# Side work on VectorE moved from in front of the row minimum to behind it, with one kind of task left in place

## The reference

```python
# 1. token encoder: embedding, e2h, six gated convolutions of width 3, h2e
for i in range(6):
    a, g = split(conv1d_same(x, conv_w[i], conv_b[i]))
    x = (a * sigmoid(g) + x) * 0.7071
h = x.T @ W_h2e + b_h2e
# 2. two attentions of 8 heads (16 wide), mixed by a gate
xn = layernorm(h)
attn1 = softmax(q1 @ k1.T / 4);  attn2 = softmax(q2 @ k2.T / 4)
stats = mean, std, max and min over windows of 4 rows of attn1 and attn2
alpha = sigmoid(mlp(stats))
h = h + (alpha * attn1 + (1 - alpha) * attn2) @ v @ Wo
# 3. normed mixture-of-experts style feed-forward
x = layernorm(layernorm(h)) * ln_g + ln_b ...;  h = h + gelu(fc2(gelu(fc1(x))) @ next_w)
```

## Time and profile before

| | |
|---|---|
| median of 3 runs | 5952.06 us (5943.18 to 5953.85) |
| the profiled execution: its own time | 5952.66 us |
| its span, first to last instruction | 5950.7 us |
| mean granted TensorE clock | 0.947 |
| TensorE matmul busy | 5237.1 us, 88% |
| VectorE busy | 5105.1 us, 86% |
| ScalarE busy | 5201.0 us, 87% |
| GpSimd busy | 2445.9 us, 41% |

### The profile page before, as it was taken

The page is one execution under the profiler, slowest core; times in us unless marked ns, Lnnn a source line. Parts: engine busy times, 40 slices in busy tenths (PEclk is TensorE's granted clock), DMA queues, the critical chain, the costliest instruction groups (busy, mean ns, idle before and its releaser), DMA issues.

```text
span 5950.7 us, 121038 instructions
## 1 busy us (share of the span) xinstructions
PE 5237.1 (88%) x34070; PEld 2513.5 (42%) x34070; DVE 5105.1 (86%) x7715; ACT 5201.0 (87%) x7937; POOL 2445.9 (41%) x4439
## 2 busy tenths in 40 slices
PE   6988989899898988989889898988989899898985
PEld 4443434444343443434344343443435344343443
DVE  2989899898998989899888988989899898989982
ACT  2998989889898999989889898998989889898893
POOL 6525344252433525344352434425353352534422
PEclk8999999999999999999999999999999999999996
DMA  1011010011101001010010101001010110101010
GB/s 38 19 23 27 18 31 20 21 27 24 27 20 29 20 21 27 20 31 19 22 28 22 27 20 28 20 23 27 22 27 20 24 24 21 27 20 30 18 23 10
DMA packets 164934, 140.87 MB, mean 24 GB/s; under 512 B 89197, under 2 KB 108269, under 8 KB 164141
## 3 DMA queue, kind: packets, MB, share of 16 engines
q1 hardware_dynamic: 159100, 124.09, 9.1%
q0 software_dynamic: 4352, 8.92, 0.7%
q10 hardware_dynamic: 816, 0.02, 0.0%
HBM read 21.26 MB, written 8.91 MB: 5 GB/s over the span
## 4 chain that ended last, share of the span: by engine, by line
PE 43%; ACT 24%; issue 15%; DVE 8%; POOL 6%; SPq 1%; ACTq 1%; DMA 1%; POOLq 0%; DVEq 0%
PE ps_w L389 19%; PE ps_t L389 10%; ACT junk L579 10%; ACT exps L586 8%; PE ps_o L389 8%; PE ps_s L389 6%; DVE neg_s L715 4%; DVE rowmin L723 2%; ACT hpre L590 2%; SPq L330 1%; DVE bn L735 1%; POOL part L866 1%; POOL ctmp L998 1%; POOL part L1000 1%; ACT L579 1%
## 5 line engine op out<-in xcount | busy, mean ns | idle before, releaser
L715 DVE TENSOR_SCALAR_CACHE_REDUCE neg_s<-ps_s 128x1024 f32<-128x1024 f32 x2048 | 2492.3, 1217 | 464.2 <-PE ps_s L389 399.0
L579 ACT ACTIVATE junk<-neg_s,negmax 128x1024 bf16<-128x1024 f32 x2048 | 2358.8, 1152 | 227.6 <-DVE neg_s L715 222.6
L723 DVE TENSOR_REDUCE rowmin<-neg_s 128x1 f32<-128x1024 f32 x2049 | 2467.3, 1204 | 0.0
L586 ACT ACTIVATE exps<-ps_t 128x1024 f32<-128x1024 f32 x2060 | 2112.6, 1026 | 171.2 <-PE ps_t L389 166.5
L389 PE MATMUL ps_t<-qst,kst 99*128 99x512 bf16 x4120 | 1300.6, 399 | 441.3 <-ACT exps L586 436.9
L389 PE MATMUL ps_o<-exps,v_cur 128*32 128x256 f32 x16512 | 1365.3, 404 | 133.2 <-DVE o_raw L731 112.2
L389 PE MATMUL ps_s<-kst,qst 96*128 96x512 bf16 x4096 | 1272.0, 392 | 65.3 <-DMA kst<-part 49.2
L389 PE MATMUL ps_w<-xc,cw 128*128 128x256 f32 x4704 | 1199.3, 392 | 1.0
L389 PEld LDWEIGHTS ps_w<-xc,cw 128*128 128x128 f32 x4704 | 922.4, 197 | 229.8 <-ACT chan L590 8.9
L866 POOL TENSOR_SCALAR ctmp<-ug 128x256 f32<-128x256 f32 x408 | 164.7, 404 | 1593.3 <-ACT ug L655 1577.9
L389 PEld LDWEIGHTS ps_t<-qst,kst 99*128 99x128 bf16 x4120 | 237.3, 98 | 1369.3 <-ACT exps L586 771.3
(11 more groups left out here) (181 smaller groups left out, 4031.4 us busy)
## 6 DMA issues: line engine op xcount, KB each, us to landing
qst<-part SPq DMA_DIRECT2D x1542, 32.0 KB, 2.0
kst<-part SPq DMA_DIRECT2D x1542, 32.0 KB, 2.0
qst<-mrow SPq DMA_DIRECT2D x1028, 1.5 KB
out_dram<-z SPq DMA_DIRECT2D x17, 512.0 KB, 3.2
fc1s<-in_fc_w SPq DMA_DIRECT2D x17, 256.0 KB
fc2s<-in_fc_w SPq DMA_DIRECT2D x17, 256.0 KB
cw<-in_conv_w SPq DMA_DIRECT2D x1, 2304.0 KB
odif<-in_table,idx POOLq DMA_INDIRECT x136
```

What stands on the lines that cost most here:

```text
L579: nc.scalar.activation(junk[:, n % 2, :], neg_s[:, n % SLOTS_S, :], ACT.Exp, scale=-1.0, bias=negmax[:, r, t:t + 1], accum_out=sumsq[:, r, ...
L586: nc.scalar.activation(exps[:, n % RING, :], ps_t[:, :, :].rearrange("p c q -> p (c q)"), ACT.Exp, scale=0.5).then_inc(s_exp, 1)
L715: nc.vector.tensor_scalar(neg_s[:, n % SLOTS_S, :], ps_s[:, n % 2, :], -1.0, None, ALU.mult, ALU.min, accum_out=negmax[:, r, t:t + 1]).the ...
L723: nc.vector.tensor_reduce(rowmin[:, r, t:t + 1], neg_s[:, m % SLOTS_S, :], axis=AX, op=ALU.max, negate=True).then_inc(s_min, 1)
```

## The change

In VectorE's loop the tasks of kind `unit` stay between `row_max` and `row_min`; all others of the step now come behind `row_min`. `plan` sorts the tasks of each step so that a `unit` stands first.

```diff
@@ plan
     for j in range(1, U + 1):
         at[j * T - 2].append(("msplit", j))
+    for n in range(STEPS):
+        at[n].sort(key=lambda task: task[0] != "unit")
     return at
@@ VectorE's loop
                     for n in range(STEPS):
                         row_max(i, n)
                         for tk in STEP[n]:
-                            task("body", i, tk)
+                            if tk[0] == "unit":
+                                task("body", i, tk)
                         row_min(i, n)
+                        for tk in STEP[n]:
+                            if tk[0] != "unit":
+                                task("body", i, tk)
```

## The result

The changed kernel takes 5885.93 us (median of 4 runs, 5878.64 to 5888.73), the kernel before on the same chip 5949.48 us (4 runs, 5943.18 to 5953.85). The ratio is 0.9892, with a 95% interval of 0.9875 to 0.9909: 1.1% faster, 63.6 us by the medians. The forecast was 5900 us, a gain of 52.3. One of nine runs of the kernel before, beside experiments 5 to 8, took 7499.44 us at a mean granted clock of 0.737 (the others 0.947 to 0.951); it is left out everywhere.

What follows compares the result with a forecast made beforehand. No engine bounds the whole, so waits were judged step by step: gains of 12.3, 13.7, 17.0, 6, 3 and 3.3 less a loss of 3 make 52.3 us, from 5952.7 to 5900 us; 8-in-10 range 5872 to 5936.

Steps and rivals of the forecast that it cites:

- Step 39, `wo`: VectorE's `wo` waits 0.77 us for TensorE; the minimum fills it all and the gain is kept: 12.3 us.
- Step 103, `h2e`: VectorE's 0.86 us wait at `h2e` goes entirely, VectorE being the pace until step 110: 13.7 us gained.
- Step 120: `mrow` waits for GpSimd near the batch's end; GpSimd's chain comes 1.06 us sooner a batch: 17.0 us gained.
- Step 8: `mrow` behind the gathering; ScalarE is the later engine in most batches: 6 us gained, bounds 0 and 16.
- Steps 16, 48, 96: `mrow`'s remaining 4 us of waits; ScalarE waits for VectorE behind 16 and 48, not 96: 3 us gained.
- `v`: Steps 123 and 124: bank freed about 1.1 us later, TensorE stands, ScalarE's spare time in step 125 covers it: 0.
- `snap` and the gate: Step 16's late reciprocal is covered by 2.0 us of slack; in steps 23 to 27 VectorE isn't the pace: 0 each.
- `next`: Step 89: 3.3 us in 16 VectorE waits, all before ScalarE's second GELU, are gained.
- the clock comes back too: Rival: TensorE's idle time before step 0 shrinks, steps 0 and 1 run at upper clock: 5883 us, chance 0.14.
- The end of the batch swallows: Rival: VectorE doesn't move the load of unit 0, so steps 103 and 120 gain nothing: 5931 us, chance 0.13.
- VectorE is covered: Rival: TensorE is the bound where VectorE idles, so only `next` and small `mrow` steps gain: 5949 us, chance 0.09.
- The bank: Rival: moved tasks free `ps_w` later and TensorE stands at `v`, `alpha` and `next`: slower, 5980 us, chance 0.07.

Runs made afterwards that it cites:

- experiment 5: The kernel before, with only `wo`, `h2e` and what stands in their steps moved behind the minimum: 5914.89 us against 5947.75, ratio 0.9948.
- experiment 6: The kernel before, with `mrow` moved behind the minimum in steps without another task, plus step 48 with `ln3`: 5924.84 us against 5947.75, ratio 0.9961.
- experiment 7: The changed kernel with both halves of `next` (steps 89 and 90) in their old place: 5866.65 us against 5947.75 before, ratio 0.9858.
- experiment 8: The changed kernel with `next` (steps 89, 90) and `v` (steps 123, 124) in their old place: 5869.24 us, ratio 0.9867 to the kernel before.
- experiment 3: The kernel before, with only the gate's `win`, `hid1` and `hid2` moved behind the minimum: 5946.66 us against 5945.66, ratio 1.0001.
- experiment 11: The kernel of experiment 7 with the norm `ln1` moved from step 108 to 109, behind that step's collection: 5871.34 us, ratio 0.9868 to the kernel before.
- experiment 9: The changed kernel with only the first half of `next` (step 89) in its old place: 5867.15 us against 5945.23 before, ratio 0.9869.

## Why the prediction was right, and where it was not

The total came out right with two terms wrong in opposite directions; that they nearly cancel is luck.

- *Step 39, `wo`* (12.3): 0.84 us a batch, 13 us. *Step 103, `h2e`* (13.7): 0.92 a batch, of which 0.23 is given back at step 112, 11 us. Together 24, and 32.9 us alone in experiment 5. Right, for the reason given: the squares behind the norms still wait 2.39 us for VectorE.
- *Step 120* (17.0): 1.10 us a batch, 17.6 us. The limit by GpSimd was the right one: `part` went from 1.30 to 0.24, the 1.06 of the forecast. `mrow` keeps 1.28 us there, some 20 in 16 batches, as forecast (19). *Step 8* (6): 0.41 a batch, 6.6 us. *Steps 16, 48, 96* (3): step 48 brings 0.29 a batch, 4.6 us, and the size is luck. Of the 4 us of waits that the forecast put here, 3.2 lie at step 96, where by its own words ScalarE doesn't wait, 0.8 at step 48 (two batches) and none at step 16. Step 48 gets shorter in every batch, from 4.93 to 4.67 us between row maxima, which the list of waits doesn't show. `mrow` alone, without step 16: 22.9 us against the forecast's 25.
- *`alpha`* (a loss of 3): nothing is lost; the shift doesn't move behind step 32. *`v`* (0): right, experiment 8.
- *`snap` and the gate* (0 and 0): here a step failed. I followed the late `snap` to ScalarE's `std` and found 2.0 us of slack, and I wrote down that the collection of step 21 would wait 1.2 us for GpSimd (it waits 1.3), but called that harmless and did not follow it to TensorE's `weighted` of step 22 and its clock. It gives 16 to 17 us. The sentence that the batches repeat each other nearly to the hundredth but for steps 8 and 9 hid it: in the trace of before the time from step 20 to step 25 already ran from 15.4 to 18.6 us from batch to batch. The gate's own tasks are worth the 0 that I took (experiment 3).
- *`next`* (a gain of 3.3): the second step that failed. The statement "all before the second GELU on ScalarE" looked at VectorE's wait alone. What its removal costs is TensorE's second half, which waits 0.67 us for the bank where I put 0.4 into a rival, and the exponential behind it: 19 us lost by the runs, 9 of them seen at this place in the traces. The Trainium skill ("Perfetto Trace Analysis", section "Optimizing Tensor Performance") advises that independent groups of matmuls rotate through PSUM banks, so that the reading of one overlaps the next. Here both halves use `ps_w`, and the trace shows the wait that the rule is against; no run here tried a second bank.

By the runs of single parts: 32.9 + 22.9 + 16, less 19, is 53 us, against 63.6 measured for all; with some 8 us of uncertainty on each number that is no contradiction, and it is not exact either.

Of the rivals, *the clock comes back too* had the nearest number, 5883 us, and the wrong place. It spoke of steps 0 and 1; the scores of step 0 run slow (over 0.7 us) in 10 batches before and in 11 after, and they still wait for the load (2.16 us before in the earlier trace rows, 2.19 after in the same batch). The clock did come back, in steps 23 and 24. The rule that the prediction weighed, of the Trainium skill ("TensorE: Matmul & The Clock Gate", section "HAM oscillation — how this bites in real kernels"), has its nearest case there: a long idle piece and slow matmuls behind it. The trace of the first batch agrees in part: the clock falls behind 1.89 us in one piece and stays up behind 0.96, but the products right behind the 1.89 us still run fast (0.61 us), so no burst starts cold there. The five batches of before that stay up with the same waits, and experiment 11, show that the pieces alone don't decide it. *The end of the batch swallows* and *VectorE is covered* fall with experiments 5 and 6. *The bank* was true of `next` and not of `v` or `alpha`.

The version that experiments 7 and 9 point to, the change without the first half of `next`, beats both kernels: 5867 us, 1.3 to 1.4% under the kernel before.

## What to carry to other kernels

Work that waits for nothing belongs ahead of work that waits, where the engine is the one others wait for: the gain can be read from the list of waits, term by term, and ends where the next engine is late. Before moving a task later, follow its result past its first reader: who waits next in the queue of that reader, and what does a PSUM bank that is freed later hold up? Of a pair of halves that shares one bank, look at what TensorE's second half holds up: the first half of `next` is better left in its old place, while those of `wo` and `h2e` gained by moving and that of `v` cost nothing, with 0.69 us to spare on ScalarE.

## What the runs showed of the hardware

A delay made the kernel faster. With TensorE's wait for the collection of step 21 some 0.8 to 0.9 us longer and its next wait shorter by as much, TensorE idles as long as before in the first batch (2.50 against 2.51 us), but its clock stays up in 10 to 15 of 16 batches instead of 5 to 9. That is worth 1.07 us a batch. The clock of one stretch also differs from batch to batch with the same waits, and from trace to trace (5 to 9 of 16 batches stay up in the five kernels with the early collection), so one trace mis-sizes such an effect: 26 us by the first pair of traces, 16 to 17 by the runs.
